# A recommendation tower on one NeuronCore: a sixteenth split step, the rest's subtraction on GpSimd, and a ring of four

## The reference, cut to what matters

```python
e = stack([tbl_f[ids[:, f]] for f in range(39)], axis=1)      # (2048, 39, 16)
x0 = xk = e
for idx, (W, b) in enumerate(params):                         # three layers of 128
    z = relu(einsum('bhd,bkd,hks->bsd', x0, xk, W) + b[None, :, None])
    if idx != 2:
        xk = z[:, :64, :]                                     # feeds the next layer
        direct.append(z[:, 64:, :])
    else:
        direct.append(z)
logit = sum(concatenate(direct, axis=1), axis=-1)             # (2048, 256)
h = concatenate([logit, dense_ctx], axis=1)
h = maximum(h @ W_top1 + b_top1, 0); h = maximum(h @ W_top2 + b_top2, 0)
return h @ W_top3
```

## Time and profile before

| | |
|---|---|
| median of 3 runs | 2515.58 us (2515.36 to 2515.76) |
| the profiled execution | 2515.79 us, of which the span is 2514.0 us |
| TensorE clock granted | 0.994 of full speed |
| busy share of the span | PE 98%, DVE 86%, POOL 74%, ACT 65%, PEld 64% |
| chain of waits, share by engine | PE 90%, POOL 3%, DVE 2%, ACT 2% |

### The profile page before, as it was taken

The page is one execution under the profiler, slowest core; times in us unless marked ns, Lnnn a source line. Parts: engine busy times, 40 slices in busy tenths (PEclk is TensorE's granted clock), DMA queues, the critical chain, the costliest instruction groups (busy, mean ns, idle before and its releaser), DMA issues.

```text
span 2514.0 us, 32633 instructions
## 1 busy us (share of the span) xinstructions
PE 2454.0 (98%) x8726; PEld 1608.1 (64%) x8726; DVE 2156.4 (86%) x1873; ACT 1644.2 (65%) x2120; POOL 1869.6 (74%) x1269
## 2 busy tenths in 40 slices
PE   5799999999999999999999999999999999999989
PEld 2466666666666666666666666666666666666655
DVE  1499899999989999999999999899999999999980
ACT  1566676767667676766767676676767667676653
POOL 6588778777877878787787778788787887865550
PEclk9899999999999999999999999999999999999999
DMA  2676667667757766866776676577667667766730
GB/s 73 136 161 149 136 148 169 134 135 163 153 124 154 157 137 136 171 142 136 152 162 137 135 167 148 122 161 155 136 140 171 139 135 156 159 135 133 169 83 0
DMA packets 214716, 352.60 MB, mean 140 GB/s; under 512 B 34382, under 2 KB 47566, under 8 KB 214588
## 3 DMA queue, kind: packets, MB, share of 16 engines
q1 hardware_dynamic: 194717, 347.07, 62.6%
q0 software_dynamic: 19968, 5.15, 2.2%
HBM read 346.97 MB, written 5.12 MB: 140 GB/s over the span
## 4 chain that ended last, share of the span: by engine, by line
PE 90%; POOL 3%; DVE 2%; issue 2%; ACT 2%; DMA 0%; ACTq 0%; DVEq 0%; POOLq 0%
PE ps L826 32%; PE ps L816 21%; PE ps L836 17%; PE ps L804 13%; PE ps L799 4%; POOL emb L379 2%; POOL Pl L385 1%; PE ps L964 1%; PE ps L792 1%; ACT Ph L520 1%; DVE P L705 1%; PE ps L956 1%; DVE ps L705 1%; DVE Pl L710 1%; PE ps L806 1%
## 5 line engine op out<-in xcount | busy, mean ns | idle before, releaser
L385 POOL TENSOR_TENSOR Pl<-P,Ph 128x1024 fp32r<-128x1024 f32 x448 | 1072.7, 2396 | 402.5 <-ACT Ph L520 399.9
L705 DVE TENSOR_TENSOR P<-xb,ps 128x1024 f32<-128x1024 f32 x768 | 924.2, 1210 | 6.7 <-ACT ps L526 5.0
L826 PE MATMUL ps<-Ph,wh 128*128 128x512 f32 x1920 | 879.1, 458 | 10.0 <-ACT Ph L520 9.9
L710 DVE TENSOR_TENSOR Pl<-ps,Ph 128x1024 fp32r<-128x1024 f32 x512 | 626.9, 1224 | 210.0 <-ACT Ph L520 197.7
L520 ACT ACTIVATE Ph<-P 128x1024 fp32r<-128x1024 f32 x448 | 473.8, 1058 | 404.9 <-DVE P L705 390.8
L379 POOL DMA_INDIRECT emb<-tbl_in,idx x624 | 599.5, 961 | 169.6 <-issue 137.3
L836 PE MATMUL ps<-Pl,wh 128*128 128x512 f32 x1920 | 701.1, 446 | 9.9 <-POOL Pl L385 9.9
L826 PE MATMUL ps<-Ph,wl 128*128 128x512 f32 x1792 | 705.3, 394 | 0.0
L520 ACT ACTIVATE Ph<-ps 128x1024 fp32r<-128x1024 f32 x512 | 522.9, 1021 | 228.2 <-DVE ps L705 224.0
L705 DVE TENSOR_TENSOR ps<-xb,ps 128x1024 f32<-128x1024 f32 x512 | 627.2, 1225 | 20.7 <-ACT ps L526 8.5
L816 PE MATMUL ps<-P,wp 128*128 128x512 f32 x1280 | 603.4, 593 | 3.5 <-DVE P L705 3.5
(11 more groups left out here) (67 smaller groups left out, 856.3 us busy)
## 6 DMA issues: line engine op xcount, KB each, us to landing
xb<-x_dram SPq DMA_DIRECT2D x1280, 256.0 KB, 8.7
emb<-tbl_in,idx POOLq DMA_INDIRECT x624
x_dram<-rows_sb SPq DMA_DIRECT2D x64, 78.0 KB
xb<-w_in SPq DMA_DIRECT2D x15, 128.0 KB
xb<-wt_in SPq DMA_DIRECT2D x2, 512.0 KB, 4.2
xb<-dense_in SPq DMA_DIRECT2D x1, 768.0 KB, 5.1
wp<-w_in SPq DMA_DIRECT2D x5, 128.0 KB
xb<-w0a_in SPq DMA_DIRECT2D x1, 448.0 KB
```

Of the source, the lines that this page charges most:

```text
L385: pool.tensor_tensor(Pl[:, h_slot(ref, c, k)], P[:, p_slot(ref, c, k)], Ph[:, h_slot(ref, c, k)], ALU.subtract).then_inc(low_pool, 1)
L705: dve.tensor_tensor(p, xb[:, x], xk.unsqueeze(1).broadcast_to([128, 2, N]), ALU.mult)\
L710: dve.tensor_tensor(Pl[:, h_slot(ref, c, k)], p_ps, Ph[:, h_slot(ref, c, k)], ALU.subtract)\
L826: pe.matmul(z_of(c, k), w[:, q, j, :], Ph[:, h_slot(ref, c, k), j, :], start=k in (L1B, L2) and i + j == 0, stop=False)
```

## The change: which engine makes which low, in which order, and three slots moved

```diff
-KIND = "GVPVGPVGVPPGVGVGVGVP"
+KIND = "VGVGVPVGVPPGVGVGVGVP"
-PRING, HRING = 4, 5
+PRING, HRING = 4, 4
-REST_AT = 19
-DIRECT0_AT, UPPER0_AT, LOWER0_AT, RELU2_AT, DIRECT1_AT, RELU1_AT = 2, 3, 4, 5, 7, 8
+REST_AT = 17
+DIRECT0_AT, UPPER0_AT, LOWER0_AT, RELU2_AT, DIRECT1_AT, RELU1_AT = 2, 3, 4, 5, 8, 8
-GATHERS = [[1, 2, 3, 5, 9, 14, 16, 18, 19], [1, 2, 3, 5, 6, 8, 9, 10],
+GATHERS = [[0, 2, 4, 5, 9, 14, 16, 18, 19], [0, 2, 4, 5, 6, 8, 9, 10],
...
+        dense0 = sb("dense0", [DX, 2 * N], F32R)
+        rows_sb, rest_sq = rows[ROWS, :], rows[LOWS, :]
...
+            def rest_low(T, chunk):
+                pool.wait_ge(rest_high, T * CPT + chunk + 1)
+                pool.wait_ge(rest_square, T * CPT + chunk + 1)
+                pool.tensor_tensor(sqx[LOWS, :], rest_sq, sqx[LOWS, :], ALU.subtract).then_inc(rest_ready, 1)
...
+                        if k == REST_AT and not (last and c >= 2):
+                            rest_low(T, c + 2)
...
                 act.activation(sqx[:, :], bank[0:REST0], ACT.Square).then_inc(rest_high, 1)
-                act.wait_ge(rest_high, T * CPT + chunk + 1)
-                act.activation(bank[LOWS], bank[LOWS], ACT.Square).then_inc(rest_square, 1)
+                act.activation(rest_sq, bank[LOWS], ACT.Square).then_inc(rest_square, 1)
...
-                        if k == REST_AT and not (last and c >= 2):
-                            rest_low(T, c + 2)
...
-                            pe.wait_ge(rest_ready, T * CPT + c + 2)
+                            pe.wait_ge(rest_square, T * CPT + c + 2)
                             transposes((c + 2) % CPT)
```

More of the change, by code:

```diff
@@ L29 @@
 LOWS = slice(0, REST)
+ROWS = slice(2 * GAP, 2 * GAP + NF)
 assert 0 < REST <= GAP
@@ L61 @@
 NEXT_IDS_AT = (2, 0)
-GATHERS = [[1, 2, 3, 5, 9, 14, 16, 18, 19], [1, 2, 3, 5, 6, 8, 9, 10],
-           [1, 2, 3, 5, 6, 9, 10, 12, 14, 16, 18, 19], [1, 2, 3, 5, 6, 8, 9, 10, 18, 19]]
+GATHERS = [[0, 2, 4, 5, 9, 14, 16, 18, 19], [0, 2, 4, 5, 6, 8, 9, 10],
+           [0, 2, 4, 5, 6, 9, 10, 12, 14, 16, 18, 19], [0, 2, 4, 5, 6, 8, 9, 10, 18, 19]]
 ORDER = [(-1, k) for k in range(L1B, L2)] + [(i, k) for i in range(CHUNKS) for k in range(STEPS)
@@ L152, in build @@
         sel0 = sb("sel0", [128, 2 * N], F32R)
-        rows_sb = sb("rows_sb", [NF, N])
+        rows = sb("rows", [ROWS.stop, N])
         sq = sb("sq", [R0, 2, N])
@@ L274, in build @@
         lo, hi = slice(0, K1), slice(K1, S)
-        FREED = (0, 2, 3, 4)
+        FREED = (0, 1, 2, 3)
         def feat_slot(s):
@@ L284, in ring_left @@
             return all_splits - HRING + 1 + FREED[s]
-        dense_left = all_splits - HRING + 2
-        dense = (Ph[0:DX, (all_splits + 1) % HRING].rearrange("p a n -> p (a n)"), sel0[0:DX, :])
+        dense = (dense0[:, :], sel0[0:DX, :])
         def feat_block(s):
@@ L305, in write_rows @@
                 sp.wait_ge(rows_ready, T * CPT + c + 1)
-                sp.dma_start(x0_dram[c % SCRATCH, 0:NF, :], rows_sb[:, :]).then_inc(rows_written, 16)
+                sp.dma_start(x0_dram[c % SCRATCH, 0:NF, :], rows_sb).then_inc(rows_written, 16)
                 sp.wait_ge(rows_written, 16 * (T * CPT + c + 1))
@@ L500, in copy_x @@
                 act.wait_ge(aux_ready, T * PER["aux"] + number + 1)
-                act.activation(rows_sb[:, :], aux_ps[0:NF], ACT.Copy).then_inc(rows_ready, 1)
+                act.activation(rows_sb, aux_ps[0:NF], ACT.Copy).then_inc(rows_ready, 1)
                 act.activation(x2[:, :], aux_ps[0:R2], ACT.Copy).then_inc(aux_read, 1)
@@ L622, in tile @@
                             act.wait_ge(dense_in, 16)
-                            act.wait_ge(split_done, dense_left)
                             for i in range(2):
@@ L711, in low, with rest_low @@
                     .then_inc(low_dve, 1)
-            def rest_low(T, chunk, bank=aux_ps):
-                dve.wait_ge(rest_square, T * CPT + chunk + 1)
-                dve.tensor_tensor(sqx[LOWS, :], bank[LOWS], sqx[LOWS, :], ALU.subtract).then_inc(rest_ready, 1)
+            def rest_low(chunk):
+                dve.wait_ge(rest_high, chunk + 1)
+                dve.wait_ge(rest_square, chunk + 1)
+                dve.tensor_tensor(sqx[LOWS, :], rest_sq, sqx[LOWS, :], ALU.subtract).then_inc(rest_ready, 1)
             dve.wait_ge(emb_high, 1)
@@ L720, in _ @@
                               emb_h[:, :, :].rearrange("p f d -> p d f"), ALU.subtract).then_inc(emb_low, 1)
-            rest_low(0, 0, early_ps[0])
+            rest_low(0)
             dve.wait_ge(xk1_ready, 1)
@@ L725, in _ @@
                 if s == 1:
-                    rest_low(0, 1)
+                    rest_low(1)
                 dve.wait_ge(xb_in[s], 32)
@@ L889, in _ @@
                 if i == 1:
-                    pe.wait_ge(rest_ready, 2)
+                    pe.wait_ge(rest_square, 2)
                 else:
@@ L893, in _ @@
                 sums(t)
+                if i == 1:
+                    pe.wait_ge(rest_ready, 2)
                 if i:
```

## The result

The changed kernel takes 2556.0 us (2555.1 to 2556.8, four runs) and the kernel before, on the same chip, 2515.7 (2515.4 to 2517.2). The ratio is 1.0159, 95% interval 1.0144 to 1.0175: **1.6% slower, by 40 us**. The forecast was 2530 us with a range of 2506 to 2546. The sign and the place were right; the size was not, and it lies outside the range.

What follows compares the result with a forecast made beforehand. The prediction took DVE's round with ACT's handovers, 36.71 us a chunk, as the bound: 42 chunks x 0.16 plus 14 x (0.16 + 0.40) is 14.5 us, added to 2515.8 gives 2530 us; 8-in-10 range 2506 to 2546.

Steps and rivals of the forecast that it cites:

- what becomes the bound: In the loop, DVE's round with ACT's work in two stretches replaces PE as bound: 36.71 us against PE's 36.19.
- PE's saving: On PE, a plain step of 1.72 us becomes a split step of 1.36: 0.36 us less per chunk, 23 us in all.
- the round of DVE and ACT is 35.36 + 0.58 + 0.77 = 36.71 us: Per chunk: DVE's own round plus waits before the lows of steps 4 and 8, 0.16 us over the old period.
- The first sum of links: ACT from product of step 2 to low of step 4: 6.64 us against DVE's 6.06, so DVE waits 0.58.
- The second sum: ACT from product of step 6 to low of step 8: 6.83 us against DVE's 6.06, so DVE waits 0.77.
- two gather stalls ... may come or go: Stalls like the 3.36 us one holding PE may change with the gathers' new places: some 8 us, in the range only.
- the second chunk of a tile,: One chunk in four: low of step 18 waits for ACT's rounding, no longer made good at step 8: 0.40 us more.
- the first and last tile, written out: Outside the loop: taken at no change, between 3 us less and 4 us more.
- PE stays the bound: Rival: the round of DVE and ACT is under 36.19 us and the kernel gets faster, 2493 us; chance 0.15.
- The handovers on ACT overlap: Rival: three handovers after roundings on ACT run 0.12 us shorter each, round 36.35 us, 2510 us; chance 0.10.
- The ring of four binds: Rival: late PE lows delay rounding 18 and the low of 18, 0.5 us a chunk, 2558 us; chance 0.07.
- What costs nothing: GpSimd's new subtraction, 0.67 to 1.32 us a chunk, moved gathers, ACT's extra rounding and the shorter ring add nothing further.

Runs made afterwards that it cites:

- The version that comes nearest to it: Changed kernel with lower half at step 5, layer 1 halves at 9, x copies at 4, rows' own buffers, gathers spread: 2491.4 us, 0.9901 of before.
- the first tile without the ring: Changed kernel with lower half at step 5, layer 1 halves at 9, ring buffers freed after high products and subtraction: 2582.0 us, 1.0259 of before.
- The run with buffers of their own: Changed kernel with the rows of x and the rest's squares each in a tensor of its own from partition 0: 2541.1 us, 1.0095 of before.
- the spread gathers: Changed kernel with gathers of a tile's first two chunks at other steps, 227 and 453 four or more steps behind their forerunners: 2544.6 us, 1.0109 of before.
- the moves: Changed kernel with layer 0's lower half at step 5 instead of 4 and both layer 1 halves at 9 instead of 8: 2524.5 us, 1.0034 of before.

## Why the prediction was right, and where it was wrong

**Right: what becomes the bound.** That DVE and ACT together take the place of PE, by ACT's work between the product of 2 and the low of 4 and between the product of 6 and the low of 8. The new waits stand at these two lows, one link taken out of one stretch gave back 30 us, and PE got waits of about 0.3 us a chunk. The prediction's own sum closes with the measured waits: 35.36 + 0.81 + 0.89, less 0.07 as the way from the low of 8 to that of 12 is 6.01 us and not 6.08, is 36.99 us, the period.

**Right: PE's saving.** 0.36 us a chunk was forecast, 36.19 us if PE bounds. The version that comes nearest to it runs at 36.13, 0.42 below before, and the first tile without the ring at 36.0. That this is somewhat more than 0.36 has a likely reason in the rows of before: twice a chunk (at 1256.14 and 1258.44) two `high` matmuls follow each other after 0.34 us where neighbours have 0.23, so PE lost about 0.2 us a chunk there too; 36.55 - 0.2 - 0.36 is 35.99, an estimate. But this saving is worth nothing until the rest is out of the way.

**Wrong: "the round of DVE and ACT is 35.36 + 0.58 + 0.77 = 36.71 us".** It is 37.0: the term for ACT's handovers was too small by 0.35 us, 1.70 in place of 0.58 + 0.77. The first sum of links came to 6.64 and measured 6.87: `upper` to the first copy, copy to copy and copy to rounding were taken as 0.58, 0.48 and 0.48, which is 1.54, and the rows have 0.68 + 0.61 + 0.50 = 1.79. The first two of these links were read from the kernel before, where the copy wrote partitions 0 to 38; the change puts it into partitions 64 to 102, which the program shows and the prediction did not read. The run with buffers of their own put 0.23 us a chunk on this alone, 13 of the 15 us that it gained. The second sum came to 6.83 and measured 6.95, mostly at "`lower` to rounding 8 0.58", now 0.67. Why is open, since that link was not varied by itself; neither the ring of four alone nor the loop is enough for it, as it stays at 0.58 to 0.59 in the kernel before with a ring of four, and is 0.67 in the changed kernel's written-out tiles too, all but the first chunk. At 56 chunks an error of 0.29 us is 16 us.

**Wrong: "two gather stalls ... may come or go" by some 8 us, kept for the range and out of the sum.** The size was right, by luck rather than from the cause: the stall was taken as one that might move, and the sign was left open. It was there to be read before: gathers 226 and 227 are 10 us apart whatever lies between, so moving the second up to the step right behind the first takes GpSimd's cover away. It cost 7.8 us, and the spread gathers took it back.

**Slightly wrong: the second chunk of a tile,** 0.34 us more in place of 0.40; and the first and last tile, written out, 2.8 us more in place of nothing (the prediction allowed up to 4). Small and of opposite sign.

**The rivals.** *PE stays the bound*: refuted; it needed the waits on ACT gone, and they went only with the moves. *The handovers on ACT overlap*: the opposite came. The rows after agree with what the prediction took from those before: `upper`, `lower` and the `direct` operations on 64 partitions start 0.02 us and more behind the end of a rounding, and the copy joined them when its target moved. By the sentence of the Trainium skill that the prediction named (page "ScalarE: Activation LUTs", section "What ACT_TABLE_LOAD costs"), they would overlap by about 93 ns like the rest; no row here shows that. *The ring of four binds*: not by itself, in the kernel before or in the changed one, whose waits for the ring grew when the kernel got faster, and where in three chunks of four no low of DVE waits at these steps. It became one part of a closed loop only after the moves.

**What costs nothing.** Held: GpSimd's subtraction took 1.27 to 1.29 us, and PE waited for it once, 0.4 us. Put back on DVE it cost 51 us more.

## What to carry to other kernels

A round that crosses two engines is a sum of links, start to start, and each link belongs to the operand's place as much as to the operation: read in the diff where every output now lies before a link is taken over. When an engine with little slack gets a link more, what counts is not its busy share but which of its instructions stand between a product and the reader who waits; moving them behind a rounding, with the gathers spread, turned 40 us lost into 25 gained. And a delay that comes at fixed counts (here at gathers 113 apart) has its price set by what is queued next to it, so look at what a moved slot leaves beside it.

## What the runs showed of the hardware that was not expected

- ACT instructions of 512 columns follow each other after 0.48 us though each lasts 0.58, but not always: the copy of 39 rows from partitions 0 to 38 into partitions 64 to 102 starts 0.68 us after its forerunner and its successor 0.61 us after it, for 0.59 and 0.48 when it writes from partition 0 on. That it is the change of partitions as such is not shown: `direct1` and `lower` write the partitions that they read and still start 0.02 us behind the end of a rounding.
- Gathers 114, 227, 453 and 566 start 4.0 to 10.3 us after the one before in all fourteen kernels (453 once 13.9), where neighbours are 1.25 us apart when nothing lies between; GpSimd's other work in between is free. They are multiples of 113 plus one; the fifth, 340, starts 7.2 to 9.4 us after its forerunner but always had enough work in between and never stood idle, so it shows no delay of its own. What the gather waits for, the profile does not show ("issue").
- With one wait more per rounding and per low, and so more instructions in the loop, ACT stopped for about 7.1 us 13 times in 14 passes, with 83 instruction packets in place of 16. That the loop's code was fetched anew each time is what this suggests; it was not tried by itself.
- A VectorE subtraction of 12 x 512 with both operands in SBUF was held up beside GpSimd, 2.4 us in place of 0.67.
